# Cross attention over 1500 keys: the values' quarter loads by an order of lanes on fifteen DMA engines, the residual's load and the result's store in slots of their own

## The chip, the cores and the metric

One core of one Trainium2 chip runs the whole program. The metric is the device time of one execution in microseconds (us); lower is better. Engines are named as the profile names them: PE (TensorE's matmuls), PEld (its weight loads), DVE (VectorE), ACT (ScalarE), POOL (GpSimd) and SP (SyncE, which issues every DMA here; SPq are its rows). The core has 16 DMA engines.

## The reference

32 samples (batches b), 56 queries and 1500 keys each, hidden size 512, 32 heads of 16. Keys and values are the same tensor `ctx`.

```python
x = (hidden - mean) * rsqrt(var + 1e-5) * gamma + beta        # layer norm over 512
Q = split_heads(x @ Wq.T); K = V = split_heads(ctx)
scores = einsum('bhsd,bhtd->bhst', Q, K) * HEAD_DIM ** -0.5
probs = softmax(where(mask, scores, -inf))                    # mask (32, 1500)
attn = einsum('bhst,bhtd->bhsd', probs, V)
out = hidden + merge_heads(attn) @ Wout.T
```

## The kernel before

**Tiles.** The 1500 keys of a batch are CHUNKS = 3 chunks of 500, and a chunk is CHUNK = 4 quarters of LANES = 125 keys, one key to a partition ("lane"). A batch has thus SLOTS = 12 slots, slot k being quarter k % 4 of chunk k // 4. The host hands the keys over transposed (`kt`) and the mask in two layouts; the values are read from `ctx` as it is: lane m of quarter k of a chunk is key 4m + k, a row of 512 floats (2048 bytes).

**The work of a slot on PE** (lines 718 to 737): four bf16 score tiles that run ahead for the next batches' maxima (`score_tile`, line 268), four matmuls that put in minus the maximum (`begin_scores`, line 301), the slot's scores in fp32 (`score_blocks`, line 309), and the product of the slot before with the values (`times_values`, line 325). DVE adds the mask to each ahead tile and takes its maximum (line 347), ACT makes the exponentials (lines 391 and 393), POOL copies a chunk's values from `v_stage` into the spread layout `v` (`spread_values`, line 435, once for four slots). Every second batch PE projects the output of a pair of batches in four parts (`project_out`, line 284), and DVE adds the residual `x_res` and leaves the sum in `result` (`add_residual`, line 364). The places are fixed in OUT_AT = [(2, 9), (3, 3), (3, 9), (4, 3)]: batches after the pair's first, and the slot.

**The work is unrolled.** The program is straight code: 40,736 matmuls with as many weight loads. There is no loop on an engine.

**SP's order** (lines 512 to 530). Before each slot SP waits until the values' product of the slot before is done (`pv_done`), then issues one quarter of the keys for two batches ahead (`load_k`, line 222: 128 partitions of 2000 bytes), one quarter of the values for the next chunk (`load_v`, line 233: 125 partitions of 2048 bytes), in slots 1, 4 and 7 a chunk of the mask (`load_mask`, line 237: 112 partitions of 1000 bytes), and in slot 4 of every even batch the result's store (`store_result`, line 247) and the residual's load (`load_residual`, line 243), both 112 rows of 2048 bytes. `v_stage` has two stages; all four quarters of a stage add 16 each to `v_landed`, for which POOL waits at line 431.

```python
if k == CHUNK and b % 2 == 0 and b > 0:
    if b > 2:
        store_result(sp, b // 2 - 2)
    load_residual(sp, b // 2 - 1)
```

Of the kernel before, what the change touches and what calls it, by code (L numbers as in the profile page):

```python
# [11 lines left out]
BATCH, QUERIES, HIDDEN = 32, 56, 512  # L12
# [6 lines left out]
BLOCKS, TILES_R, ROW = 4, 4, 32  # L19
# [2 lines left out]
BANK_Q = BLOCKS * PAIR_Q  # L22
CHUNKS, CHUNK, LANES = 3, 4, 125
SLOTS = CHUNKS * CHUNK
KEYS = CHUNK * LANES
MAX_TILES = CHUNKS * PAIRS
AHEAD = 8
# [3 lines left out]
STAGES = 2  # L31
# [42 lines left out]
def slot_units(b, k):  # L74

    tiles = slot_tiles(b, k)
    return tiles[0:3] + slot_rows(b, k) + tiles[3:4] + slot_others(b, k)
# [3 lines left out]
RING = FIRST_TILES + [("rows", 0)]  # L81
RING += [unit for b in range(BATCH) for k in range(SLOTS) for unit in slot_units(b, k)]
LAST_OUTS = [("out", d, part) for d in range(BATCH // 2 - 2, BATCH // 2) for part in range(OUT_PARTS)]
# [5 lines left out]
def build(nc, x, kt, ctx, mask_lanes, mask_rows, wq_t, wout_t, gamma, beta, out):  # L89
    with ExitStack() as stack:  # L90
        def sb(name, shape, dt=F32):
            return stack.enter_context(nc.sbuf_tensor(name, shape, dt))

        def sem(name):
            return stack.enter_context(nc.semaphore(name))
# [4 lines left out]
        v_stage = sb("v_stage", [128, STAGES, CHUNK, HIDDEN])  # L100
# [5 lines left out]
        woutT = sb("woutT", [128, BLOCKS, HIDDEN])  # L106
        mask_bias = sb("mask_bias", [128, BATCH * SLOTS])
        mask_tile = sb("mask_tile", [128, 2, CONTEXT], BF16)
        masked = sb("masked", [128, len(RING_BANKS), KEYS], BF16)
        tile_max = sb("tile_max", [128, CHUNKS, PAIRS])  # L110
# [22 lines left out]
        ln_weights = sb("ln_weights", [128, 2, BLOCKS])  # L133
        lanes_u8 = sb("lanes_u8", [128, BATCH * SLOTS], U8)
        rows_u8 = sb("rows_u8", [BATCH, CONTEXT], U8)
# [6 lines left out]
        def x_tile(t):  # L142
            if t < 14:
# [3 lines left out]
              for i in range(2)]  # L147
        wqT = v_scratch[:, 2 * BLOCKS * BANK_Q:2 * BLOCKS * BANK_Q + BLOCKS * HIDDEN].rearrange("p (c n) -> p c n",
                                                                                              c=BLOCKS)
# [23 lines left out]
        v_landed = [sem(f"v_landed{i}") for i in range(STAGES)]  # L173
# [27 lines left out]
        def wait_over(eng, semaphore, count):  # L201
            if count > 0:
                eng.wait_ge(semaphore, count)
# [4 lines left out]
        def wait_taken(eng, unit):  # L208
            eng.wait_ge(ring_taken, RING_AT[unit] + 1)
# [11 lines left out]
        def load_k(sp, b, c, g):  # L221
            sp.dma_start(kT[:, b % 2, c, g].rearrange("p k m -> p (k m)"), kt[b, c, :, KEYS * g:KEYS * (g + 1)]
                         ).then_inc(k_landed[b % 2][c], 16)
# [3 lines left out]

        def load_v(sp, b, c, k):
            n = CHUNKS * b + c
            src = ctx[b, KEYS * c:KEYS * (c + 1), :].rearrange("(m k) n -> m k n", k=CHUNK)  # L230
            if k == 0:
                wait_over(sp, v_ready, n - STAGES + 1)
            sp.dma_start(v_stage[0:LANES, n % STAGES, k], src[:, k]).then_inc(v_landed[n % STAGES], 16)

        def load_mask(sp, b, c):
            keys = slice(KEYS * c, KEYS * (c + 1))
            sp.dma_start(mask_tile[0:PAIR_Q, b % 2, keys], mask_add[b:b + 1, keys].broadcast_to([PAIR_Q, KEYS])
                         ).then_inc(mask_tile_landed[b % 2], 16)
# [6 lines left out]
        def store_result(sp, d):  # L245
            wait_taken(sp, ("out", d, OUT_PARTS - 1))
            sp.dma_start(out_rows[d], result[0:PAIR_Q, :]).then_inc(result_stored, 16)
# [8 lines left out]
        def score_tile(pe, unit):  # L256
# [5 lines left out]
            if t % PAIRS == 0:  # L262
# [4 lines left out]
            keys = keys.rearrange("p (n h) -> p n h", h=2)[:, :, 1]  # L267
            nc.tensor.matmul(bank[0:PAIR_Q, 0:KEYS], qdb[rows, b % 2, g, :], keys,  # L268
                             start=True, stop=True).then_inc(ring_filled, 1)
# [19 lines left out]
        def begin_scores(pe, b, k):  # L289
# [3 lines left out]
            if k == 0:  # L293
                pe.wait_ge(rows_spread, b + 1)
                pe.wait_ge(qd_ready, b + 1)
            n = SLOTS * b + k
            wait_over(pe, exped_held, n)
# [7 lines left out]
        def score_blocks(pe, b, k, blocks):  # L305
            for g in blocks:
                for r in range(TILES_R):
                    rows = slice(ROW * r, ROW * (r + 1))
                    mm = nc.tensor.matmul(ps[0:LANES, score_bank(SLOTS * b + k, r), PAIR_Q * g:PAIR_Q * (g + 1)],  # L309
                                          kT[rows, b % 2, k // CHUNK, g, k % CHUNK, :], qd[rows, b % 2, g, :],  # L310
# [4 lines left out]
        def times_values(pe, b, k):  # L315
            c = k // CHUNK
            if k % CHUNK == 0:
                pe.wait_ge(v_ready, CHUNKS * b + c + 1)
            pe.wait_ge(exped, SLOTS * b + k + 1)
            if k == 0:  # L320
# [107 lines left out]
        def spread_values(pool, b, c):  # L428

            n = CHUNKS * b + c  # L430
            pool.wait_ge(v_landed[n % STAGES], 16 * CHUNK * (n // STAGES + 1))
            wait_over(pool, pv_done, CHUNK * (n - CHUNKS + 1))
            halves = v[0:LANES, c].rearrange("p k i (h d) -> p (k i) h d", d=HEAD_DIM)[:, :, 0:3:2, :]
            staged = v_stage[0:LANES, n % STAGES].rearrange("p k (i h d) -> p (k i) h d", h=2, d=HEAD_DIM)
            nc.gpsimd.tensor_copy(halves, staged).then_inc(v_ready, 1)  # L435
# [33 lines left out]
        @block.sync  # L469
        def _(sp):  # L470
            def load_x(u):
                for t in range(UNIT_AT[u], UNIT_AT[u] + UNIT_TILES[u]):
                    sp.dma_start(x_tile(t), x_rows[t]).then_inc(x_landed[u], 16)

            load_x(0)
            for n, weight in enumerate((gamma, beta)):
                sp.dma_start(ln_weights[:, n, :], weight.rearrange("(c p) -> p c", p=128),
                             allow_slow_non_contiguous=True).then_inc(ln_landed, 16)
            sp.dma_start(wqT, wq_t.rearrange("(c p) n -> p c n", p=128)).then_inc(wq_landed, 16)
            sp.dma_start(rows_u8[:, :], mask_rows).then_inc(mask_landed, 16)  # L480
            sp.dma_start(lanes_u8[0:LANES, :], mask_lanes).then_inc(mask_landed, 16)
            load_x(1)
            for g in range(BLOCKS):
                load_k(sp, 0, 0, g)
            for u in range(2, UNITS):
                load_x(u)
            for g in range(BLOCKS):
                load_k(sp, 0, 1, g)
            for g in range(BLOCKS):
                load_k(sp, 0, 2, g)  # L490
            sp.wait_ge(mask_added, 1)
            sp.dma_start(mask_add, rows_add[:, :]).then_inc(mask_stored, 16)
            for g in range(BLOCKS):
                load_k(sp, 1, 0, g)
            sp.wait_ge(mask_stored, 16)
            for c in range(CHUNKS):
                load_mask(sp, 0, c)
            for c in range(CHUNKS):
                load_mask(sp, 1, c)
            for k in range(CHUNK):  # L500
                load_v(sp, 0, 0, k)
            sp.dma_start(woutT[:, :, :], wout_t.rearrange("(c p) n -> p c n", p=128)).then_inc(wout_landed, 16)
            for g in range(BLOCKS):
                load_k(sp, 1, 1, g)
            for g in range(BLOCKS):
                load_k(sp, 1, 2, g)
            sp.wait_ge(filled, FILLS)
            for k in range(CHUNK):
                load_v(sp, 0, 1, k)
            for k in range(CHUNK):  # L510
                load_v(sp, 0, 2, k)
            for b in range(BATCH):
                for k in range(SLOTS):
                    step = k % CHUNK
                    wait_over(sp, pv_done, SLOTS * b + k)
                    if (b, k) >= (0, CHUNK):
                        of, c = (b + 2, k // CHUNK - 1) if k >= CHUNK else (b + 1, CHUNKS - 1)
                        if of < BATCH:
                            load_k(sp, of, c, step)
                        of, c = (b + 1, k // CHUNK - 1) if k >= CHUNK else (b, CHUNKS - 1)  # L520
                        if of < BATCH:
                            load_v(sp, of, c, step)
                    if k in (1, 4, 7) and b + 2 < BATCH:
                        if k == 1:
                            wait_taken(sp, ("tile", b, MAX_TILES - 1))
                        load_mask(sp, b + 2, k // 3)
                    if k == CHUNK and b % 2 == 0 and b > 0:
                        if b > 2:
                            store_result(sp, b // 2 - 2)
                        load_residual(sp, b // 2 - 1)  # L530
            store_result(sp, BATCH // 2 - 2)
            load_residual(sp, BATCH // 2 - 1)
            store_result(sp, BATCH // 2 - 1)
            sp.wait_ge(result_stored, 16 * (BATCH // 2))
# [249 lines left out]
```

## Time and profile before

| | us |
|---|---|
| median of 3 runs | 1495.26 (1488.03 to 1503.92) |
| profiled execution | 1497.4 |
| its span, first to last instruction | 1495.6 |
| granted TensorE clock over the span | 0.963 |
| PE busy / PEld / DVE | 1352.0 / 1037.6 / 1088.4 |
| ACT / POOL | 769.7 / 388.8 |

The span is 1.8 us shorter than the execution's own time. Busy times are sums over the span; the clock is a share of 2.4 GHz, and it is granted at one of two levels, 2.4 or 1.2 GHz. An idle time is put down to what ended it; "issue" is an idle time for which the profile shows nothing that was waited for.

### The profile page before, as it was taken

How to read it: one execution, taken by the hardware profiler on the slowest of the kernel's cores; microseconds unless marked ns; L12 is line 12 of the kernel's file. 1: busy time of each engine (PE TensorE's matmuls, PEld its weight loads, DVE VectorE, ACT ScalarE, POOL GpSimd, SP SyncE). 2: the span in 40 equal slices, each digit the busy share in tenths (PEclk: the TensorE clock that was granted, in tenths of full speed). 3: DMA queues.
4: the chain of work that ended last, by engine and by line, in shares of the span. 5: the costliest groups of instructions: out<-in, count | busy, mean ns of one | idle time of the engine just before them, and what ended most of it. 6: DMA issues, size and time to landing. Idle time of an engine off the chain costs nothing.

```text
span 1495.6 us, 88664 instructions
## 1 busy us (share of the span) xinstructions
PE 1352.0 (90%) x40736; PEld 1037.6 (69%) x40736; DVE 1088.4 (73%) x3452; ACT 769.7 (51%) x847; POOL 388.8 (26%) x371
## 2 busy tenths in 40 slices
PE   6999989999999989999999989989998998889986
PEld 4347777777667777777777767767776777677775
DVE  6657778788777777877777877878786777777640
ACT  2126555555555555555455555555554554555463
POOL 1011323332322233322222332322223222223221
PEclk8999999999999999999999999999999999999899
DMA  8314555555545544555555554555555444454430
GB/s 271 99 38 150 163 160 160 161 159 159 166 152 162 166 156 154 161 163 158 156 158 173 162 161 150 167 153 161 170 166 153 145 151 158 147 170 145 131 98 21
DMA packets 126358, 226.37 MB, mean 151 GB/s; under 512 B 11619, under 2 KB 71555, under 8 KB 125987
## 3 DMA queue, kind: packets, MB, share of 16 engines
q1 hardware_dynamic: 125986, 220.71, 47.7%
q8 instruction: 320, 5.24, 1.5%
q14 instruction: 52, 0.42, 0.1%
HBM read 216.90 MB, written 3.77 MB: 148 GB/s over the span
## 4 chain that ended last, share of the span: by engine, by line
PE 66%; DVE 26%; issue 6%; ACT 2%; DMA 0%; POOL 0%; SPq 0%; POOLq 0%; DVEq 0%; ACTq 0%
DVE masked L347 22%; PE ps L325 22%; PE ps L268 21%; PE ps L309 12%; PE ps L284 5%; PE ps L707 4%; PE ps L301 2%; DVE den_inv L383 2%; ACT probs L391 1%; PE ps L275 1%; DVE tile_max L347 1%; DMA v<-in_wq_t 0%; DVE probs L612 0%; PE ps L698 0%; DVE den L376 0%
## 5 line engine op out<-in xcount | busy, mean ns | idle before, releaser
L347 DVE CUSTOM_DVE_ANT_0 masked<-ps,mask_tile 112x500 bf16<-112x500 f32 x1536 | 974.1, 674 | 327.4 <-PE ps L268 315.1
L391 ACT ACTIVATE probs<-ps,mask_bias 125x1344 f32<-125x1344 f32 x384 | 530.6, 1382 | 629.6 <-PE ps L309 629.6
L268 PE MATMUL ps<-kT,qdb 32*112 32x500 bf16 x1536 | 496.6, 423 | 45.5 <-DVE tile_max L347 35.8
L309 PE MATMUL ps<-qd,kT 32*125 32x112 f32 x12288 | 478.7, 277 | 13.6 <-issue 13.4
L309 PEld LDWEIGHTS ps<-qd,kT 32*125 32x125 f32 x12288 | 475.1, 190 | 21.7 <-issue 18.0
L325 PE MATMUL ps<-probs,v 125*32 125x56 f32 x24576 | 410.4, 218 | 38.0 <-issue 36.1
L325 PEld LDWEIGHTS ps<-probs,v 125*32 125x32 f32 x24576 | 343.7, 113 | 132.7 <-issue 125.5
L268 PEld LDWEIGHTS ps<-kT,qdb 32*112 32x112 bf16 x1536 | 156.3, 125 | 208.2 <-DVE tile_max L347 158.9
L393 ACT ACTIVATE probs<-ps,mask_bias 125x448 f32<-125x448 f32 x384 | 240.7, 627 | 0.0
L435 POOL COPY v<-v_stage 125x2048 f32<-125x2048 f32 x96 | 181.7, 1892 | 201.1 <-DMA v_stage<-in_ctx 201.1
L301 PE MATMUL ps<-max_rows,ones_row 4*125 4x448 bf16 x1536 | 213.7, 391 | 7.9 <-ACT probs L391 5.5
L424 POOL TENSOR_TENSOR max_rows<-rows,own_block 128x448 bf16<-128x448 f32 x32 | 29.9, 934 | 613.3 <-DVE rows L370 613.3
L347 DVE DVE_READ_ACCUMULATOR2_ANT tile_max<- 112x1 f32 x1536 | 127.9, 83 | 0.0
L464 POOL TENSOR_TENSOR attnT<-heads,den_inv 128x224 f32<-128x224 f32 x32 | 21.1, 658 | 248.3 <-DVE den_inv L383 248.3
L284 PE MATMUL ps<-woutT,attnT 128*112 128x128 f32 x512 | 74.2, 291 | 7.5 <-POOL attnT L464 4.8
L284 PEld LDWEIGHTS ps<-woutT,attnT 128*112 128x112 f32 x512 | 61.7, 183 | 22.3 <-DVE tile_max L347 11.6
L301 PEld LDWEIGHTS ps<-max_rows,ones_row 4*125 4x125 bf16 x1536 | 64.5, 132 | 15.3 <-ACT probs L391 6.7
L707 PE MATMUL ps<-v 128*128 128x448 f32 (+2 forms) x160 | 66.1, 534 | 2.5 <-DMA v<-in_wq_t 1.5
L383 DVE RECIPROCAL den_inv<-den 128x56 f32<-128x56 f32 x128 | 63.1, 496 | 0.2
L364 DVE TENSOR_TENSOR result<-ps,x_res 112x128 f32<-112x128 f32 x64 | 18.6, 291 | 40.0 <-PE ps L284 36.6
L672 ACT COPY qT<-ps 128x448 f32<-128x448 f32 (+2 forms) x20 | 9.1, 457 | 64.6 <-PE ps L707 64.5
L707 PEld LDWEIGHTS ps<-v 128*128 128x128 f32 x160 | 27.5, 216 | 18.2 <-issue 12.5
(48 smaller groups left out, 295.6 us busy)
## 6 DMA issues: line engine op xcount, KB each, us to landing
kT<-in_kt SPq DMA_DIRECT2D x384, 250.0 KB, 3.1
v_stage<-in_ctx SPq DMA_DIRECT2D x384, 250.0 KB
mask_tile<-mask_add SPq DMA_DIRECT2D x96, 109.4 KB, 4.5
x_res<-in_x SPq DMA_DIRECT2D x16, 224.0 KB, 5.6
out<-result SPq DMA_DIRECT2D x16, 224.0 KB, 5.4
probs<-in_x SPq DMA_DIRECT2D x14, 224.0 KB, 8.4
v<-in_wq_t SPq DMA_DIRECT2D x1, 1024.0 KB, 6.0
woutT<-in_wout_t SPq DMA_DIRECT2D x1, 1024.0 KB, 16.9
```

Source lines behind the costliest of these rows:

```text
L268: nc.tensor.matmul(bank[0:PAIR_Q, 0:KEYS], qdb[rows, b % 2, g, :], keys, start=True, stop=True).then_inc(ring_filled, 1)
L284: mm = nc.tensor.matmul(bank[0:PAIR_Q, 0:OUT_COLS], attnT[:, d % 2, g, :], woutT[:, g, OUT_COLS * part:OUT_COLS * (part + 1)], start=(g == ...
L301: nc.tensor.matmul(ps[0:LANES, score_bank(n, r), 0:BANK_Q], ones_row[rows, :], max_rows[rows, b % 2].rearrange("p g n -> p (g n)"), start= ...
L309: mm = nc.tensor.matmul(ps[0:LANES, score_bank(SLOTS * b + k, r), PAIR_Q * g:PAIR_Q * (g + 1)], kT[rows, b % 2, k // CHUNK, g, k % CHUNK, ...
L325: mm = nc.tensor.matmul(acc[ROW * r:ROW * (r + 1), i, :], v[0:LANES, c, k % CHUNK, TILES_R * g + r, HEAD_DIM * e:HEAD_DIM * e + ROW], prob ...
L347: nc.vector.tensor_tensor_reduce(out=sums, in0=bank[0:PAIR_Q, 0:KEYS], in1=mask_tile[0:PAIR_Q, b % 2, KEYS * c:KEYS * (c + 1)], scale=1.0, ...
L383: nc.vector.reciprocal(den_inv[:, g], den[:, g]).then_inc(den_inverted, 1)
L391: nc.scalar.activation(probs[0:LANES, k % PROBS, 0:HELD_ROWS], ps[0:LANES, 0:HELD_ROWS, 0:BANK_Q], ACT.Exp, bias=bias, scale=SCALE).then_i ...
L393: nc.scalar.activation(probs[0:LANES, k % PROBS, HELD_ROWS], ps[0:LANES, score_bank(n, HELD_ROWS), 0:BANK_Q], ACT.Exp, bias=bias, scale=SC ...
L424: nc.gpsimd.tensor_tensor(max_rows[:, b % 2], rows[:].unsqueeze(1).broadcast_to([128, BLOCKS, PAIR_Q]), own_block[:].unsqueeze(2).broadcas ...
L435: nc.gpsimd.tensor_copy(halves, staged).then_inc(v_ready, 1)
L707: mm = nc.tensor.matmul(bank, wqT[:, h, 128 * c:128 * (c + 1)], xT[u % 2][:, h, 0:w], start=(h == 0), stop=(h == BLOCKS - 1))
```

## The change

The 125 lanes of a quarter are put in another order. The first 120 are read as 8 rows of 15: lane a*8 + j holds the key row that was lane 15j + a; the last five stay. So a quarter's load becomes two DMAs: one with a source of 15 x 8 rows for lanes 0 to 119, and one for lanes 120 to 124. The host puts the transposed keys and both layouts of the mask in the same order. `v_landed` now gets 32 per quarter. SP issues the store in slot 5 and the residual's load in slot 6, in place of both in slot 4.

```diff
+VALUE_RINGS = 15
+EVEN_LANES = LANES // VALUE_RINGS * VALUE_RINGS
+LANE_OF = [m for a in range(VALUE_RINGS) for m in range(a, EVEN_LANES, VALUE_RINGS)] + list(range(EVEN_LANES, LANES))
...
         def load_v(sp, b, c, k):
             n = CHUNKS * b + c
-            src = ctx[b, KEYS * c:KEYS * (c + 1), :].rearrange("(m k) n -> m k n", k=CHUNK)
+            src = ctx[b, KEYS * c:KEYS * (c + 1), :].rearrange("(m k) n -> m k n", k=CHUNK)[:, k]
+            even = src[0:EVEN_LANES].rearrange("(j a) n -> a j n", a=VALUE_RINGS)
             if k == 0:
                 wait_over(sp, v_ready, n - STAGES + 1)
-            sp.dma_start(v_stage[0:LANES, n % STAGES, k], src[:, k]).then_inc(v_landed[n % STAGES], 16)
+            sp.dma_start(v_stage[0:EVEN_LANES, n % STAGES, k], even).then_inc(v_landed[n % STAGES], 16)
+            sp.dma_start(v_stage[EVEN_LANES:LANES, n % STAGES, k], src[EVEN_LANES:LANES]
+                         ).then_inc(v_landed[n % STAGES], 16)
...
-            pool.wait_ge(v_landed[n % STAGES], 16 * CHUNK * (n // STAGES + 1))
+            pool.wait_ge(v_landed[n % STAGES], 2 * 16 * CHUNK * (n // STAGES + 1))
...
-                    if k == CHUNK and b % 2 == 0 and b > 0:
-                        if b > 2:
-                            store_result(sp, b // 2 - 2)
+                    if k == CHUNK + 1 and b % 2 == 0 and b > 2:
+                        store_result(sp, b // 2 - 2)
+                    if k == CHUNK + 2 and b % 2 == 0 and b > 0:
                         load_residual(sp, b // 2 - 1)
...
-    keys = ctx.reshape(BATCH, CHUNKS, LANES, CHUNK, BLOCKS, 128)
-    lanes = mask.reshape(BATCH, CHUNKS, LANES, CHUNK)
+    keys = ctx.reshape(BATCH, CHUNKS, LANES, CHUNK, BLOCKS, 128)[:, :, LANE_OF]
+    lanes = mask.reshape(BATCH, CHUNKS, LANES, CHUNK)[:, :, LANE_OF]
```

## Rows read from the trace of the kernel before

**Rows 1.** The page: busy times, and the chain that ended last by engine.

```profile
PE 1352.0 (90%) x40736; PEld 1037.6 (69%) x40736; DVE 1088.4 (73%) x3452; ACT 769.7 (51%) x847; POOL 388.8 (26%) x371
...
PE 66%; DVE 26%; issue 6%; ACT 2%; DMA 0%; POOL 0%; SPq 0%; POOLq 0%; DVEq 0%; ACTq 0%
```

**Rows 2.** Waits: engine line <- releaser, us in total, times, longest us.

```profile
POOL v L435 <- DMA v_stage<-in_ctx: 201.1, 36, 30.0
PEld ps L325 <- issue: 125.5, 388, 2.8
PE ps L325 <- issue: 36.1, 44, 2.7
PE ps L309 <- issue: 13.4, 24, 2.3
PE ps L301 <- issue: 2.1, 3, 1.1
```

**Rows 3.** Engines by stretch: the whole loop, then four single batches.

```profile
core 0: us, PE busy (x) PEld busy (x) DVE busy (x) ACT busy (x) POOL busy (x), PEclk, DMA share, GB/s
161.40:1415.40 1254.00, 1147.83 (x36586) 901.76 (x36585) 957.78 (x3059) 673.43 (x723) 346.32 (x318) 0.97 0.52 158
...
933.90:974.30 40.40, 37.95 (x1267) 29.80 (x1267) 32.93 (x107) 23.34 (x26) 11.97 (x11) 1.00 0.53 165
974.30:1019.90 45.60, 40.83 (x1267) 31.81 (x1266) 33.24 (x107) 23.41 (x26) 11.97 (x11) 0.93 0.52 156
1019.90:1061.40 41.50, 39.02 (x1267) 30.41 (x1266) 33.31 (x107) 23.25 (x26) 11.97 (x11) 1.00 0.51 161
1326.40:1371.90 45.50, 40.17 (x1267) 31.84 (x1266) 33.39 (x107) 23.27 (x26) 12.01 (x11) 0.96 0.49 156
```

**Rows 4.** Timeline of PE: first, one middle and last of eleven stalls.

```profile
208.89 1.53 PE L325 MATMUL ps<-probs,v 125*32 125x56 f32 x55 [2.66 <-issue]
...
725.98 0.62 PE L325 MATMUL ps<-probs,v 125*32 125x56 f32 x19 [1.42 <-issue]
...
1156.96 1.41 PE L309 MATMUL ps<-qd,kT 32*125 32x112 f32 x21 [2.33 <-issue]
```

**Rows 5.** The page: DMA queues, packets, MB, share of 16 engines.

```profile
q1 hardware_dynamic: 125986, 220.71, 47.7%
q8 instruction: 320, 5.24, 1.5%
```

**Rows 6.** Timeline of SP around the stall at 724.56 us.

```profile
718.08 0.35 SPq L222 DMA_DIRECT2D kT<-in_kt  x1
718.47 0.33 SPq L233 DMA_DIRECT2D v_stage<-in_ctx  x1
718.84 0.32 SPq L237 DMA_DIRECT2D mask_tile<-mask_add  x1
719.20 0.43 SPq L247 DMA_DIRECT2D out<-result  x1
719.97 0.33 SPq L243 DMA_DIRECT2D x_res<-in_x  x1
721.75 0.35 SPq L222 DMA_DIRECT2D kT<-in_kt  x1
722.15 0.33 SPq L233 DMA_DIRECT2D v_stage<-in_ctx  x1
```

**Rows 7.** Engines by short stretch: values alone; burst's middle; burst's end; after the stall.

```profile
715.90:716.90 1.00, 1.00 (x35) 0.89 (x31) 0.97 (x3) 0.00 (x0) 0.00 (x0) 1.00 0.32 123
...
720.40:721.90 1.50, 1.50 (x71) 1.15 (x75) 1.09 (x4) 1.50 (x2) 1.50 (x2) 1.00 0.46 147
722.20:723.20 1.00, 1.00 (x37) 0.75 (x29) 1.00 (x3) 0.00 (x0) 0.12 (x1) 1.00 0.86 243
...
725.90:733.00 7.10, 7.02 (x157) 6.21 (x159) 3.86 (x12) 1.91 (x2) 0.00 (x0) 0.52 0.44 128
```

**Rows 8.** DMA issues: KB each, median us from issue to landing.

```profile
kT<-in_kt SPq DMA_DIRECT2D x384, 250.0 KB, 3.1
v_stage<-in_ctx SPq DMA_DIRECT2D x384, 250.0 KB
mask_tile<-mask_add SPq DMA_DIRECT2D x96, 109.4 KB, 4.5
x_res<-in_x SPq DMA_DIRECT2D x16, 224.0 KB, 5.6
out<-result SPq DMA_DIRECT2D x16, 224.0 KB, 5.4
```

**Rows 9.** Timeline of SP in a stretch with no stall.

```profile
961.19 0.35 SPq L222 DMA_DIRECT2D kT<-in_kt  x1
961.58 0.33 SPq L233 DMA_DIRECT2D v_stage<-in_ctx  x1
964.26 0.35 SPq L222 DMA_DIRECT2D kT<-in_kt  x1
964.65 0.33 SPq L233 DMA_DIRECT2D v_stage<-in_ctx  x1
```

## The prediction

> **What bounds the kernel now.** I read the page first. PE is busy 90% of the span, DVE 73%, and the chain that ended last is 66% PE, 26% DVE, 6% "issue" and 0% DMA [rows 1]. By that view a change to loads is worth nothing: no engine on the chain waits for a transfer, and POOL, which does wait 201.1 us for the values, is busy 26% and copies four slots ahead of need [rows 1, 2]. So the question became what the 6% of issue is, some 90 us in which PE waited for nothing that the profile shows.
>
> The second view was the loop by batches. The issue of the keys' load in slot 4 marks each batch; from 161.4 to 1415.4 us there are 29 of them. One (933.9 to 974.3) took 40.40 us at a full clock; the next 45.60 us at a clock of 0.93, with the same instructions and the same busy time on DVE, ACT and POOL [rows 3]. So 40.4 us is what the code needs by its own waits, and 29 x 40.4 = 1171.6 us against 1254.0 leaves 82.4 us of disturbance in the loop. That is what a change to DMAs can reach.
>
> The third view was PE's timeline in the bad batches. Eleven times PE stops for 1.24 to 2.66 us, mostly in the middle of a run of matmuls of one line, where there is no semaphore to wait for [rows 4]. Then the granted clock is at its lower level for a stretch: 725.9 to 733.0 us shows 0.52 [rows 7], 1.2 GHz for nearly all of it. All idle time of PE before a matmul that is put down to issue sums to 36.1 + 13.4 + 2.1 = 51.6 us [rows 2]. The loop's clock of 0.97 [rows 3] is (1 - 0.97) x 1254 = 38 us of work done late. 52 + 38 = 90 us, the size of the 82 found by batches.
>
> **What PE waits for there.** The program is straight code, and the page has a queue of kind instruction: 320 packets, 5.24 MB, thus 16.4 KB each [rows 5]. PE and PEld have 81,472 instructions [rows 1], 255 to a packet. PE's code thus comes by DMA, a block every 4 us or so, and a stop within a run of one line is a block that is late. The trace names no engine for it, so this is an inference.
>
> The Trainium skill ("Runtime: NRT & Kernel Launch", Instruction fetch mechanics) says the same of the size, 16 KiB blocks of 256 instructions, and that crossing one is mostly hidden. By that rule the stops are something else and the time would stay where it is; the rows with stops of up to 2.66 us inside a run speak against "hidden" in this program, so I give it a small chance below.
>
> Why late? Ten of the eleven stops come in the slot after the one in which SP issues keys, values, mask, result and residual in a row (the first without a result yet), the eleventh one slot later; one such burst stands at 718.08 to 719.97 us, and its stop from 724.56 to 725.98 [rows 4, 6]. The DMA share tells more. While only a quarter of values moves, the engines' mean share is 0.32 at 123 GB/s: five of sixteen [rows 7]. 250 KB at 123 GB/s is 2.1 us on those five. In the burst's middle (720.4 to 721.9) the share is still only 0.46, though mask, result and residual have been issued and go over all engines; only when the values are through does it rise to 0.86 [rows 7]. So what stands behind the values in SP's queue is let out at the pace of the five engines while others idle, and SP itself is held: the residual is issued 0.77 us after the result where neighbours are 0.37 apart [rows 6]. The code block, I think, is held up in the same jam. The mask's 109 KB take 4.5 us to land against 3.1 for the keys' 250 KB [rows 8]: the same jam, small, in three slots of each batch.
>
> **The change part by part.**
>
> *Values on fifteen engines.* The Trainium skill ("DMA: Bandwidth & Descriptors", Why a DMA increments its semaphore by 16 and not by 1) has the engine count as the largest divisor up to 16 of both sides' slowest dimension: 5 for 125, 15 for 15 x 8 rows into 120 partitions. The trace agrees on the 5.
> If the split works, a quarter has 8 rows to an engine in place of 25, and 2.1 x 8/25 = 0.7 us in place of 2.1. The last five lanes add one row on each of some engines, under 0.1 us. The jam behind the values goes, in every slot.
>
> *One more issue per slot on SP.* 384 more issues at 0.33 us plus the gap, about 0.37 us each. A slot's issues become 0.4 + 0.4 + 0.4 + 0.4 (mask) = 1.6 us within a slot of 3.08 us in which nothing disturbs (keys at 961.19 and at 964.26) [rows 9]. SP waits for the rest anyway. On the path: 0. If SP were to fall behind, values land four slots before their use and keys a batch before; the cover is over 10 us. Bounds: 0 to 2 us. The larger count at line 431 costs nothing.
>
> *Order of lanes.* Host work, and the same rows in SBUF; softmax sums over lanes in another order. PE, DVE, ACT and POOL issue what they did. 0.
>
> *Store in slot 5, residual in slot 6.* Neither slot has a mask. The residual is used in slot 9, three slots or 9 us later, and takes 5.6 us [rows 8]; the result's store takes 5.4 us and `result` is written again in slot 9. Both hold. The moved pair no longer stands with the mask behind one set of values: 2.1 us on five engines plus three transfers become, per slot, keys and values and one transfer of at most 224 KB over 16 engines. Nothing new is waited for; 0 on SP.
>
> *Sum.* The eleven long stops are 21.6 us (2.66 + 1.72 + 1.75 + 1.24 + 2.59 + 1.56 + 1.42 + 1.25 + 2.57 + 2.50 + 2.33; first and last in [rows 4]). The lower clock, 38 us, follows them; the batch from 1019.9 to 1061.4 us, with short stops alone, has 1.00 [rows 3]. I take all of the stops and 32 of the 38, since a few lower stretches may stay: 54 us. The short stops are 51.6 - 21.6 = 30 us, of which some 6 lie in head and tail; late batches such as 1326.4 to 1371.9 (45.50 us) are full of them [rows 3]. Those behind a mask or a tail of values should go; those behind the keys' load, which takes all 16 engines as before, stay. I take a third off, 8 us. 1497.4 - 54 - 8 = 1435.4; for the second issue and new meetings I add 3 and say 1438 us. The profiled run is 2.1 us above the median of three, within their spread of 16 us, so nothing is taken off for that. Both ends: all 82 us gone and some more in head and tail gives 1412; nothing gained gives 1497.
>
> **The rivals.**
>
> 1. *Only the long stops' worst part goes.* If the code block is delayed by any busy engines, and the jam is only part of it, keys and values together still hold it. Then stops shrink from 2 to 1 us and half of the clock comes back: 1497 - 11 - 19 = 1467 us. For it: short stops occur in batches without store or residual [rows 3]. Against: the batch at 933.9 has five-engine values throughout and no loss.
>
> 2. *No effect.* Either the load stays on five engines, or the stops belong to the fetch itself, whatever else moves. 1490 to 1500 us. For it: 0% of the chain is DMA [rows 1], and one long stop, at 208.89 us, has no store before it. Against: the stops' place, one slot after the burst.
>
> 3. *Slower.* The code block comes over engines that values do not touch today; from the change on they carry 0.7 us of values behind 0.7 to 1 us of keys in each slot. If a block waits for both, every one is up to 0.7 us later. Where the slack is gone (PE stopped before a matmul 44 + 24 + 3 = 71 times [rows 2] for 320 blocks), that is some 80 x 0.5 us = 40 us more, partly met by what the moved store and residual give (20 us): 1517 us. It decides if the block's engine serves SP's packets first; for it speaks that the values' own stretch shows no sign of sharing, 0.32 at 123 GB/s; against it, that DMA share is 0.53 on the mean and a block moves 16 KB in about 1.1 us (1.5% x 16 x 1495.6 / 320) [rows 5].
>
> **How the numbers follow.** The forecast with 1412 to 1455 us gets 0.60, rival 1 0.19, rival 2 0.13, rival 3 0.08. The range of 8 in 10 is 1410 to 1482. About 1% is what a measurement of this kernel can tell from no change; faster by more takes the forecast and nearly all of rival 1: 0.79; within 1% 0.14; slower 0.07.
>
> **What would show it.** Right: while only values move, a DMA share near 0.9 for 0.7 us in place of 0.32 for 2.1; two issues of `v_stage` to a slot; the mask landing in about 3 us in place of 4.5; PE's idle time from issue before a matmul from 51.6 to under 25 us; the loop's clock at 0.99 or more; batches of 40.4 to 42 us, even and odd alike; DVE, ACT and POOL busy as before. Wrong: stops of over 1.2 us that stay in the slots after 4, 5 or 6 of even batches (rival 1 or 2), or more short stops in every batch and a block's packet time well over 1.1 us (rival 3).

## The result: slower by 1.9%, and the profile after

The changed kernel takes 1524.76 us (median of 4 runs, 1517.77 to 1532.55) against 1497.78 for the one before in the same comparison: ratio 1.0188, 95% interval 1.0107 to 1.0268. The forecast was 1438 with a range of 1410 to 1482; the result lies outside it, on the other side of no change. The profiled execution took 1528.94 us, its span 1526.7. Ratios here and below leave out executions over 1.5% above the fastest one of the same kernel (none of these four, five of the ten of padded below), medians do not.

From the page of the changed kernel: busy times, queues, the chain by engine, DMA issues with the median us to landing.

```profile
PE 1360.0 (89%) x40736; PEld 1040.7 (68%) x40736; DVE 1087.7 (71%) x3452; ACT 770.0 (50%) x847; POOL 388.5 (25%) x371
...
q1 hardware_dynamic: 131746, 220.73, 52.0%
q8 instruction: 320, 5.24, 1.4%
...
PE 66%; DVE 24%; issue 7%; ACT 1%; DMA 0%; POOL 0%; SPq 0%; POOLq 0%; DVEq 0%; ACTq 0%
...
kT<-in_kt SPq DMA_DIRECT2D x384, 250.0 KB, 3.3
v_stage<-in_ctx SPq DMA_DIRECT2D x384, 240.0 KB
mask_tile<-mask_add SPq DMA_DIRECT2D x96, 109.4 KB, 3.5
v_stage<-in_ctx SPq DMA_DIRECT2D x384, 10.0 KB
x_res<-in_x SPq DMA_DIRECT2D x16, 224.0 KB, 4.0
out<-result SPq DMA_DIRECT2D x16, 224.0 KB, 3.4
```

The engines do the same work [rows 1]. Mask, residual and result land 1.0, 1.6 and 2.0 us sooner than before [rows 8], as forecast. The packets grew by 5760 = 384 x 15 [rows 5], and the trace has them as packets of 4 bytes, 11,493 before and 17,253 now. That fits one such packet from each engine that takes part in a DMA: a quarter now ends on 15 + 5 in place of 5 engines, and the spread does what it says. But the same 220.7 MB keep the sixteen engines busy for 52.0% of a longer span in place of 47.7%.

The waits of PE and SP (engine line <- releaser, us in total, times, longest us); L331 and L315 are the values' product and the scores, [rows 2] of before.

```profile
POOL v L441 <- DMA v_stage<-in_ctx: 181.3, 37, 23.7
PEld ps L331 <- issue: 149.9, 426, 2.6
PE ps L331 <- issue: 53.9, 75, 2.4
PE ps L315 <- issue: 14.7, 30, 1.0
PE ps L307 <- issue: 2.1, 4, 1.1
```

PE's idle time before a matmul for which the profile shows nothing was 51.6 us in 71 stops; it is 53.9 + 14.7 + 2.1 = 70.7 us in 109. They are a little shorter (0.65 us on the mean against 0.73) and far more. They make up 19.1 of the 31.1 us by which the span grew; PE's busy time, 1360.0 against 1352.0, makes up 8.0. Three batches of after and the whole loop by stretch show the same, as [rows 3] did.

```profile
core 0: us, PE busy (x) PEld busy (x) DVE busy (x) ACT busy (x) POOL busy (x), PEclk, DMA share, GB/s
164.40:1400.40 1236.00, 1115.29 (x35436) 872.98 (x35440) 928.02 (x2966) 652.66 (x700) 335.00 (x308) 0.98 0.57 156
204.50:251.90 47.40, 41.86 (x1267) 32.89 (x1266) 33.29 (x107) 23.16 (x26) 12.01 (x11) 0.93 0.54 146
1008.00:1049.30 41.30, 38.58 (x1267) 29.84 (x1266) 33.09 (x107) 23.44 (x26) 11.96 (x11) 1.00 0.61 173
1354.20:1400.40 46.20, 39.57 (x1270) 30.86 (x1273) 33.79 (x109) 23.81 (x27) 11.99 (x11) 1.00 0.57 154
```

The last of these batches runs at a full clock and still takes 46.20 us: PE's idle time put down to issue is 4.6 us in it and 0.3 us in the one at 1008.0. The best one takes 41.30, the best before 40.40. The loop's clock is 0.98 against 0.97, so the clock is not what made the kernel slower; nor did it come back to 0.99, where I had counted on 32 of its 38 us.

What became of a quarter of values is read from 702.4 to 704.2 us of after, in two parts and whole, with SP's issues around it, and from a later quarter with no mask behind it (709.9 to 711.4 us).

```profile
702.40:703.10 0.70, 0.68 (x26) 0.45 (x30) 0.70 (x3) 0.70 (x1) 0.70 (x2) 1.00 0.72 50
703.10:704.20 1.10, 1.10 (x68) 1.02 (x59) 0.51 (x3) 0.94 (x2) 1.10 (x1) 1.00 0.71 253
702.40:704.20 1.80, 1.78 (x77) 1.47 (x80) 1.21 (x5) 1.64 (x2) 1.80 (x2) 1.00 0.71 174
709.90:711.40 1.50, 1.50 (x79) 1.39 (x82) 0.91 (x5) 1.34 (x2) 0.00 (x0) 1.00 0.48 150
```

```profile
700.16 0.36 SPq L225 DMA_DIRECT2D kT<-in_kt  x1
700.57 1.23 SPq L237 DMA_DIRECT2D v_stage<-in_ctx  x1
701.83 0.47 SPq L238 DMA_DIRECT2D v_stage<-in_ctx  x1
702.36 0.32 SPq L243 DMA_DIRECT2D mask_tile<-mask_add  x1
703.83 0.35 SPq L225 DMA_DIRECT2D kT<-in_kt  x1
704.23 0.87 SPq L237 DMA_DIRECT2D v_stage<-in_ctx  x1
705.14 0.46 SPq L238 DMA_DIRECT2D v_stage<-in_ctx  x1
```

For 0.7 us 72% of the engines are busy and move 50 GB/s: many have begun a row and few bytes arrive. The quarter takes some 1.8 us, not 0.7. Its second part is not the values' alone: the mask issued at 702.36 starts to move at 703.6 us, and without a mask the share is 0.48. The cost in engine time is better read from the trace's packets over the whole loop (165 to 1400 us). A packet of 2048 bytes, nearly always a row of values, takes 116.5 ns on the mean against 89.5 before; the median is 84 in both, so it is a tail of slow ones. A quarter's 125 rows thus hold 14.6 us of engine time in place of 11.2. The queue's shares agree: 0.520 x 16 x 1526.7 us is 1288 us more than 0.477 x 16 x 1495.6, 3.4 us for each of the 384 quarters. I had counted 0.7 us on fifteen engines, no more engine time than before. The issue itself went from 0.33 us to 0.87 + 0.47, which the experiments had to clear or convict.

### The profile page after: what moved, and what is told of

Read it like the earlier page. It is cut to its first block, busy times and chain, and to the rows that moved or that the text cites. A ratio compares the mean times of both kernels' runs of the same rounds, so it can differ in the third digit from the quotient of the medians.

```text
span 1526.7 us, 89048 instructions
## 1 busy us (share of the span) xinstructions
PE 1360.0 (89%) x40736; PEld 1040.7 (68%) x40736; DVE 1087.7 (71%) x3452; ACT 770.0 (50%) x847; POOL 388.5 (25%) x371
## 2 busy tenths in 40 slices
DMA packets 132120, 226.41 MB, mean 148 GB/s; under 512 B 17378, under 2 KB 77314, under 8 KB 131746
## 3 DMA queue, kind: packets, MB, share of 16 engines
q1 hardware_dynamic: 131746, 220.73, 52.0%
## 4 chain that ended last, share of the span: by engine, by line
PE 66%; DVE 24%; issue 7%; ACT 1%; DMA 0%; POOL 0%; SPq 0%; POOLq 0%; DVEq 0%; ACTq 0%
PE ps L331 22%; DVE masked L353 22%; PE ps L274 20%; PE ps L315 12%; PE ps L290 5%; PE ps L713 4%; PE ps L307 2%; DVE den_inv L389 1%; PE ps L281 1%; ACT probs L397 1%; DVE tile_max L353 1%; DMA v<-in_wq_t 0%; PE ps L704 0%; DVE probs L618 0%; DVE den L382 0%
## 5 line engine op out<-in xcount | busy, mean ns | idle before, releaser
L274 PE MATMUL ps<-kT,qdb 32*112 32x500 bf16 x1536 | 492.9, 421 | 47.7 <-DVE tile_max L353 39.8
L315 PE MATMUL ps<-qd,kT 32*125 32x112 f32 x12288 | 480.6, 276 | 14.8 <-issue 14.7
L315 PEld LDWEIGHTS ps<-qd,kT 32*125 32x125 f32 x12288 | 475.8, 189 | 24.1 <-issue 20.5
L331 PE MATMUL ps<-probs,v 125*32 125x56 f32 x24576 | 419.6, 218 | 56.1 <-issue 53.9
L331 PEld LDWEIGHTS ps<-probs,v 125*32 125x32 f32 x24576 | 347.2, 112 | 157.6 <-issue 149.9
```

What stands on the lines that cost most here:

```text
L331: mm = nc.tensor.matmul(acc[ROW * r:ROW * (r + 1), i, :], v[0:LANES, c, k % CHUNK, TILES_R * g + r, HEAD_DIM * e:HEAD_DIM * e + ROW], prob ...
```

## The experiments

Ratios are against the kernel before, timed on the same chip in the same comparison. "Idle" is PE's idle time before matmuls put down to issue, the values', the scores' and the maximum's lines summed from each profile as above.

| kernel | engines for the values' bulk, rows' order, DMAs per quarter | ratio (95% interval) | median us | idle us |
|---|---|---|---|---|
| before | 5, old, 1; slot 4 | 1 | | 51.6 |
| after | 15, changed, 2 | 1.0188 (1.0107 to 1.0268) | 1524.76 | 70.7 |
| slots | 5, old, 1 | 0.9852 (0.9799 to 0.9905) | 1480.99 | 38.7 |
| rings | 15, changed, 2; slot 4 | 1.0280 (1.0214 to 1.0346) | 1543.12 | 82.2 |
| natural | 15, old, 2 | 1.0079 (1.0030 to 1.0129) | 1512.90 | 53.9 |
| five_two | 5, changed, 2 | 1.0188 (1.0131 to 1.0245) | 1529.43 | 69.5 |
| one_plain | 15, old, 1 | 1.0079 (1.0044 to 1.0114) | 1510.72 | 54.2 |
| one_3d | 15, changed, 1 | 1.0196 (1.0123 to 1.0269) | 1533.57 | 71.8 |
| narrow | 15, changed, 2, 1/8 of the bytes | 0.9694 (0.9650 to 0.9739) | 1456.67 | 32.6 |
| five_plain | 5, old, 2 | 0.9861 (0.9810 to 0.9911) | 1481.54 | 36.2 |
| ten | 10, old, 2 | 0.9824 (0.9770 to 0.9879) | 1471.00 | 34.7 |
| eleven | 11, old, 2 | 0.9915 (0.9878 to 0.9952) | 1492.18 | 42.6 |
| thirteen | 13, old, 2 | 0.9996 (0.9964 to 1.0028) | 1502.14 | 50.0 |
| split15 | 15, old, 2 | 1.0041 (0.9998 to 1.0085) | 1503.29 | 57.0 |
| split5 | 15 (meant: 5), old, 2 | 0.9998 (0.9954 to 1.0042) | 1501.82 | 55.8 |
| padded | 15, near old, 2, form kept | 1.0022 (0.9978 to 1.0066) | 1511.91 | 55.0 |
| keys_eleven | 10, old, 2; keys on 11 | 0.9931 (0.9886 to 0.9976) | 1492.72 | 42.4 |
| whole_keys | 5, old, 1; keys once a chunk | 1.0381 (1.0307 to 1.0456) | 1554.83 | 74.9 |
| apart15 | 15, old, 2; half a slot later | 1.0132 (1.0092 to 1.0173) | 1526.86 | 63.1 |
| apart10 | 10, old, 2; half a slot later | 1.0020 (0.9978 to 1.0063) | 1507.71 | 55.4 |

All but "before" and the "slot 4" row have the store and the residual in slots 5 and 6. In five_plain the last ten lanes are a DMA of their own, on ten engines by the count of packets. The idle column goes with the ratio nearly all the way: a kernel whose loads cost more has more stops of PE that the profile cannot put down to a semaphore. They are not the whole difference. PE's busy time moves too, from 1329.5 us in narrow to 1378.2 in rings, while the granted clock of the span goes from 0.988 to 0.950. natural, split15 and split5 came out as the same loads (below) and gave 1.0079, 1.0041 and 0.9998 in two comparisons, so steps of less than about 0.008 between kernels of different comparisons say little.

**Half and half.** The change has two parts; each was run alone.

slots:

```diff
-                    if k == CHUNK and b % 2 == 0 and b > 0:
-                        if b > 2:
-                            store_result(sp, b // 2 - 2)
+                    if k == CHUNK + 1 and b % 2 == 0 and b > 2:
+                        store_result(sp, b // 2 - 2)
+                    if k == CHUNK + 2 and b % 2 == 0 and b > 0:
                         load_residual(sp, b // 2 - 1)
```

> The kernel before with only the store moved to slot 5 and the residual's load to slot 6. Jam theory (transfers behind the five-engine values hold the code block): the stops after even batches' slot 4 shrink, 1465 to 1480 us, ratio 0.98 to 0.99. Rival (the move itself is harmful or idle): ratio 1.00 or above.

rings is the changed kernel with these lines as they were.

> The changed kernel with store and residual back in slot 4: fifteen engines alone. If the fifteen engines carry the whole loss and the slots gain: above the changed kernel, 1535 to 1550 us. If the slots carry the loss: 1500 us or below.

The slots gain 1.5%, some 22 us, and the values' load loses it and more, with or without them: 1.0280 against 1, 1.0188 against 0.9852. The two parts add within their intervals. In the trace of slots the longest stop before a values' matmul is 1.6 us against 2.7 before.

```profile
PE ps L325 <- issue: 22.6, 46, 1.6
PE ps L309 <- issue: 13.0, 23, 1.1
PE ps L301 <- issue: 3.1, 5, 1.1
```

```profile
mask_tile<-mask_add SPq DMA_DIRECT2D x96, 109.4 KB, 4.6
x_res<-in_x SPq DMA_DIRECT2D x16, 224.0 KB, 5.9
out<-result SPq DMA_DIRECT2D x16, 224.0 KB, 4.9
```

Mask and residual land no sooner in slots than before (4.5 and 5.6 us there; the result took 5.4), and it gains all the same; the changed kernel lands all three sooner and loses. The time to landing is no measure of what the code meets on the engines.

**What in the values' load?** Three things had changed at once: engines, order of rows with a dearer issue, and a second DMA.

natural (changed kernel, two lines):

```diff
-LANE_OF = [m for a in range(VALUE_RINGS) for m in range(a, EVEN_LANES, VALUE_RINGS)] + list(range(EVEN_LANES, LANES))
+LANE_OF = list(range(LANES))
...
-            even = src[0:EVEN_LANES].rearrange("(j a) n -> a j n", a=VALUE_RINGS)
+            even = src[0:EVEN_LANES]
```

> The changed kernel with the lanes in their old order: lanes 0 to 119 as a plain block of 120 rows, and lanes 120 to 124. If 120 rows also go over fifteen engines with an issue of 0.33 us in place of 0.87, issue theory (the code block waits while SP's issues are made into descriptors): 1495 to 1510 us. Engine theory (values on the block's own engine hold it): 1520 to 1530 us like the changed kernel.

five_two (changed kernel with 5 for VALUE_RINGS and 120 for EVEN_LANES):

> The changed kernel with 5 in place of 15 (24 rows to an engine, the last five lanes in a second DMA as there): the dear form and the second issue stay, the spread goes. Issue theory: 1515 to 1530 us like the changed kernel. Engine theory: the ratio of the kernel with moved slots alone, 0.98 to 1.00.

Changed order, dear form and second DMA on five engines cost as much as the whole load on fifteen, 1.0188, and natural, with its cheaper issues, lies between. That read as a win for the issue theory, by which the code waits while SP makes its issues. The issues' own durations (min/median/max ns): natural, then five_two.

```profile
L237 SPq DMA_DIRECT2D v_stage<-in_ctx x384: 324/440/1887, 31.8 to 1473.0; - x192
L238 SPq DMA_DIRECT2D v_stage<-in_ctx x384: 289/299/690, 32.3 to 1473.3; - x192
```

```profile
L237 SPq DMA_DIRECT2D v_stage<-in_ctx x384: 753/759/896, 35.7 to 1487.5; - x192
L238 SPq DMA_DIRECT2D v_stage<-in_ctx x384: 477/487/772, 36.6 to 1488.3; - x192
```

**The issue theory tested.** one_plain and one_3d drop the second DMA from natural and from the changed kernel:

```diff
-            sp.dma_start(v_stage[EVEN_LANES:LANES, n % STAGES, k], src[EVEN_LANES:LANES]
-                         ).then_inc(v_landed[n % STAGES], 16)
+            if n < STAGES:
+                sp.dma_start(v_stage[EVEN_LANES:LANES, n % STAGES, k], src[EVEN_LANES:LANES]
+                             ).then_inc(v_landed[n % STAGES], 16)
```

The count that POOL waits for follows. Both kernels leave out the last five lanes of every quarter after the first two chunks, 4% of the values' bytes.

> Natural order, fifteen engines, one DMA per quarter: lanes 120 to 124 are loaded for the first two chunks alone and keep their old values later (4% of the values' bytes left out). Issue theory (SP 0.35 + 0.44 us a slot): 1481 to 1492 us, like the kernel with moved slots alone. Engine theory: 1505 to 1515 us, like the natural order with both DMAs.

> The changed kernel's order of lanes, one DMA per quarter, lanes 120 to 124 left out after the first two chunks. If SP's time per issue decides (0.35 + 0.87 = 1.22 us a slot): 1500 to 1512 us. If the number of issues decides: 1481 to 1492 us. If the spread over engines decides: 1520 us.

five_plain is natural with EVEN_LANES = 115:

> Moved slots, natural order, each quarter as lanes 0 to 114 and lanes 115 to 124: the bulk stays on five engines, one plain issue of some 0.3 us is added. Issue theory: 1500 to 1515 us, as the natural order on fifteen engines. If the second issue costs nothing by itself: 1475 to 1485 us.

narrow is the changed kernel with

```diff
+            cols = slice(0, HIDDEN if n < STAGES else HIDDEN // 8)
-            sp.dma_start(v_stage[0:EVEN_LANES, n % STAGES, k], even).then_inc(v_landed[n % STAGES], 16)
+            sp.dma_start(v_stage[0:EVEN_LANES, n % STAGES, k, cols], even[:, :, cols]).then_inc(v_landed[n % STAGES], 16)
```

and the same columns in the second DMA. It leaves out 7/8 of the values' bytes after the first two chunks.

> The changed kernel with the same DMAs and rows, but after the first two chunks only the first 64 of 512 columns of each value row are loaded (256 bytes in place of 2048; the other columns keep old values). Issue theory: 1515 to 1530 us, unchanged. Traffic theory (the bytes on the engines hold the code block): below 1495 us.

Here the issue theory fell. A second issue is free: one_plain equals natural (1.0079 both), one_3d equals the changed kernel, five_plain equals slots. narrow keeps every issue at its full price and is the fastest kernel of the study, with the loop's clock at 1.00. The rows that decide: narrow's issues, its queue and its loop.

```profile
L238 SPq DMA_DIRECT2D v_stage<-in_ctx x384: 872/882/1892, 33.0 to 1417.6; - x192
L239 SPq DMA_DIRECT2D v_stage<-in_ctx x384: 457/468/614, 34.1 to 1418.5; - x192
```

```profile
q1 hardware_dynamic: 131746, 136.50, 34.8%
```

```profile
161.40:1400.00 1238.60, 1147.56 (x37327) 895.48 (x37327) 976.33 (x3125) 686.73 (x737) 348.17 (x320) 1.00 0.37 99
```

So it is what the values' bytes do on the engines. One_plain and five_plain have the same plain form and differ in the spread of the bulk: 15 engines cost 0.022 more than 5.

**How many engines?** ten, eleven and thirteen are natural with EVEN_LANES at 100, 121 and 117.

> Moved slots, natural order, plain form, each quarter as lanes 0 to 99 on ten engines (10 rows each) and 100 to 124 on five. Engine theory with the code block on one of the upper five that the values reach at fifteen (10 to 14): ratio 0.985 as on five engines. With the block on one of 5 to 9: 1.008 as on fifteen. With the block's engine changing from block to block: about 0.997.

> Moved slots, natural order, lanes 0 to 120 on eleven engines (11 rows each), 121 to 124 on four. One-engine theory: 0.982 as on ten, unless the code's engine is the eleventh, then 1.005. Slope theory (each further engine costs a little): about 0.987.

> Lanes 0 to 116 on thirteen engines (9 rows each), 117 to 124 on eight. One-engine theory: 0.982 if the code's engine is the 14th or 15th, 1.005 if it is the 11th to 13th. Slope theory: about 0.996.

Ten engines cost nothing (0.9824, within the interval of five). Then it climbs: 0.9915 and 0.9996, in one comparison and with intervals that do not meet, and 1.0049 as the mean of natural, one_plain, split15 and split5, the old order on fifteen. The last step, from thirteen to fifteen, is within what such kernels differ by. Eleven lies between the 0.987 of the slope theory and the 1.005 of a single engine that is the eleventh; thirteen, which is above eleven, speaks for the slope. The number of rows to an engine and the second DMA's engines change along with the count, so the slope is one of all three. keys_eleven asks the same from the other side, taking the keys off the upper engines too:

```diff
-            sp.dma_start(kT[:, b % 2, c, g].rearrange("p k m -> p (k m)"), kt[b, c, :, KEYS * g:KEYS * (g + 1)]
-                         ).then_inc(k_landed[b % 2][c], 16)
+            for lo, hi in ((0, 110), (110, 128)):
+                sp.dma_start(kT[lo:hi, b % 2, c, g].rearrange("p k m -> p (k m)"), kt[b, c, lo:hi, KEYS * g:KEYS * (g + 1)]
+                             ).then_inc(k_landed[b % 2][c], 16)
```

> Values on ten engines as in the run of that name, and the keys' quarter in two DMAs, partitions 0 to 109 on eleven engines (10 rows each), 110 to 127 on nine. If the code's engine is the 12th to 15th it now carries mask, result and residual alone: most stops go, clock 0.99, 1420 to 1445 us. If it is the 11th, or if any engine's traffic holds the code: 1465 to 1480 us.

The count that PE waits for follows. 1492.72 us is 0.011 above ten and above both of the ranges given: taking the keys off the upper engines gained nothing. It also adds an issue to each slot and puts more on the engines that are left, so it tells only that no upper engine is worth keeping free of keys; with the slope it is against a single one.

**The order of rows.** split15 and split5 read `"(a j) n -> a j n"` in place of `"(j a) n -> a j n"`; padded does so with one row of padding after every eight in the source, so that the form stays.

> The changed kernel, its three-dimensional form of source kept (15 x 8 rows), but each engine reads eight neighbouring rows, so the lanes stay in their old order. If the form costs (SP 0.87 us an issue): 1.019 as the changed kernel. If the order of addresses costs: 1.008 as the plain form on fifteen. Should SP's issue come back to 0.44 us the form has been folded and only the latter can be seen.

> The same on five engines (5 x 24 neighbouring rows and five lanes). Form theory: 1.019 as with the changed order on five engines. Address theory: 0.985 as the plain form on five.

> The changed kernel's two DMAs on fifteen engines with its 15 x 8 form kept by one row of padding after every eight in the values' source; each engine reads neighbouring rows. Form theory: 1.019 as the changed kernel. Address theory: 1.005 as the natural order on fifteen.

Both splits were folded back into the plain form: their issues take 435 and 436 ns like natural's, and both count 131746 packets, the number of fifteen engines, split5 too. So neither tells form from addresses, and split5 is a third run of natural's loads, which is why it stands at 15 in the table. padded tells it: its issue takes 883 ns, as the changed kernel's, and its ratio is 1.0022.

```profile
L237 SPq DMA_DIRECT2D v_stage<-in_ctx x384: 872/883/1867, 31.5 to 1464.7; - x192
```

On fifteen engines the form is free, and the changed order of addresses costs: 1.0188 and 1.0196 against 0.9998 to 1.0079. (The padding moves the rows' addresses too; which property of them counts is not shown.) On five engines the order with its form costs 0.033 (five_two against five_plain); there the form was not tried apart. And with the changed order fifteen engines are no dearer than five, 1.0188 both. So spread and order do not add: the order with its form, alone on five engines, brings the whole loss of 0.033, and the spread alone 0.020 of it.

**Is it the length of a burst?** whole_keys loads a chunk's keys at once, in rows of 8000 bytes (K_STEP is 2; the count that PE waits for follows):

```diff
-            sp.dma_start(kT[:, b % 2, c, g].rearrange("p k m -> p (k m)"), kt[b, c, :, KEYS * g:KEYS * (g + 1)]
+            if g != K_STEP:
+                return
+            sp.dma_start(kT[:, b % 2, c].rearrange("p g k m -> p (g k m)"), kt[b, c]
                          ).then_inc(k_landed[b % 2][c], 16)
```

> Moved slots, values as before on five engines; the keys of a chunk come in one DMA of 1 MB (8000 bytes a partition) in place of four, issued at the third of its four slots. If the keys' 16-engine bursts of 1.1 us in every slot are what is left of the stops: fewer stops but longer ones, 1450 to 1480 us. If a long burst holds a block for all of its 3 us: 1490 to 1520 us.

1554.83 us, the slowest of all and above its rival's range of 1490 to 1520: one burst of 1 MB in four slots, with a quarter of the issues, is worse than four of 250 KB. apart15 and apart10 go the other way and part keys and values:

```diff
                         if of < BATCH:
+                            sp.wait_ge(scored, SLOTS * b + k + 2)
                             load_v(sp, of, c, step)
```

> Natural order on fifteen engines, but SP waits for the next slot's scores between the keys' and the values' issue, some 1.4 us. If the joined stretch of keys and values holds the code: ratio down from 1.005 to 0.985 or below. If the amount of traffic decides: 1.00 to 1.008, unchanged.

> The same on ten engines. Joined stretch: from 0.982 down to 0.965 to 0.975. Amount: 0.98 to 0.985. Should the wait make values late, POOL's wait for them would pass 250 us and PE would wait for the spread values.

Both lost, 0.008 and 0.020 against their parents (1.0049 and 0.9824), and both lie above everything expected of them; the first difference is at the edge of what comparisons differ by. Two separate bursts per slot are worse than one joined, though the wait also holds back mask, result and residual. So the joined stretch is not what costs; a longer burst (whole_keys) and more bursts (apart) both do, fewer bytes help (narrow).

**What the stops wait for.** The kept traces hold the packets of the queue "instruction" with their times, 320 of 16 KB [rows 5], and these settle it for the long stops. In the loop of the kernel before (165 to 1400 us) PE stops, with neither a matmul nor a weight load, for more than 1.2 us eleven times. Each of these stops ends 1.2 to 1.6 us after such a packet has ended, and the next packet starts 1.1 to 1.8 us after the stop. Over the 20 kernels there are 146 such stops, and each ends 1.2 to 1.8 us behind a packet's end, where a packet starts only every 4.2 us at the median. So a long stop is PE waiting for its code, and it ends when a block has come. There are 11 before, 9 in after, 13 in rings, 11 in five_two, 21 in whole_keys, and one each in slots, ten and narrow. (The many shorter stops are not sorted out as cleanly.)

The delay lies ahead of the packet and not in it. The eleven late packets take 1.04 us on the mean, those of the whole loop 1.12, but they start 5.9 to 7.1 us after the one before them, against the median of 4.2. In the 1.5 us before they start, the loads' packets keep the engines 87% busy, against 50% before an average code packet (77% against 54% in after). Over all 20 kernels it is 76% against 52%. The reading that fits all of this, though no run isolates it, is that a code packet has to wait for quiet engines, and each arrangement of the loads leaves more or less of them. What it waits for there, a descriptor, an engine's turn or memory, and over which engines it comes, no run here tells.

## Why the prediction was wrong

**What bounds the kernel: right.** The disturbance was in PE's unexplained stops, and they moved the time in both directions, from 0.9694 to 1.0381, with DMA at 0 or 1% of the chain throughout. That they are waits for code was an inference from the size and number of the packets; for the long ones the packets' times show it. The Trainium skill ("Runtime: NRT & Kernel Launch", Instruction fetch mechanics) calls this cost mostly hidden; by these rows it is not in this program, where 220 MB of loads run beside straight code.

**Slots 5 and 6: right.** They gain 1.5% alone, within the 0.98 to 0.99 expected of them, and leave one stop of over 1.2 us of eleven. The burst of five transfers in one slot was the trouble, as the prediction has it.

**The jam: right as a fact, wrong as the cause.** Mask, residual and result do land sooner. But in the spread kernels no time followed from it. The step that failed is "The code block, I think, is held up in the same jam": that the five engines' stretch of values holds the code, so that ending it early gives back 54 + 8 us. The runs show the reverse: with the old order, fifteen engines cost 30 us over five, and with the changed order nothing was gained by them. Under it lies a second failed step, "if the split works, a quarter has 8 rows to an engine in place of 25, and 2.1 x 8/25 = 0.7 us". The quarter read above took some 1.8 us, and a quarter holds 14.6 us of engine time in place of 11.2, as a row takes 116.5 ns in place of 89.5; I had kept the engine time as a constant. What I had read as waste, eleven idle engines for 2 us of each slot, was probably of use: the runs with ten to fifteen engines say so, though none shows which engine brings the code.

**The terms.** Spread to fifteen: +2.0% or 30 us (1.0049 against 0.985 for five), forecast as part of a gain of 62. Order of rows: +1.4% or 21 us (1.0188 against 1.0049), forecast 0: the prediction calls it "Host work" and leaves out that the engines read other addresses. Slots: -22 us. The sum, +29 us, meets the measured 1524.76 - 1497.78 = 27. It does so by the path taken: with the order changed first, on five engines, order and form cost 49 us (1.0188 against 0.9861) and the spread then 0. Only their sum, some 50 us, is firm. The second issue, for which I had set 0 to 2 us, is free, as costed. That last point is worth its place: SP's 1.7 us per slot looked like a culprit and was none.

**The rivals.** Rival 3 came nearest, at a chance of 0.08: more stops, each short, 1517 us; there were 38 more stops and 1524.76 us. That the number is so near is partly luck: it had +40 for the spread and nothing for the order. Its argument, that values would reach engines that the code had to itself, fits the runs from ten to fifteen engines in the old order. It does not explain five_two, which loses the same on five engines, and one of its signs did not come: a code packet takes 1.08 us on the mean and not well over 1.1 (1.12 before). The code comes late and not slowly. I ranked the rival low because the batch at 933.9 us ran well with the spread as it was, which spoke for the five engines and not for fifteen. Of my signs for a right forecast the mask's landing came near (3.5 us for about 3); the DMA share near 0.9 for 0.7 us, the loop's clock of 0.99 and the idle time (under 25 us forecast, 70.7 found) did not come. The idle time tells the two apart at one look.

## What to carry to other kernels

A transfer that nobody waits for can still set the time through the engines it keeps busy: before spreading a load, ask who else uses the engines that it does not touch, the program's own code included, and read the idle time that the profile puts down to issue. Spread only as far as it helps: here ten engines with plain rows and the slots moved is the best that was built, 1471.00 us (0.9824), 3.6% under the changed kernel by their ratios, though its interval meets those of five engines. Where one edit bundles a count, an order and a form, try each by itself; here the part that looked dear (SP's issues) was free, and one that looked free (the order of rows) cost 21 us on fifteen engines. Where a stop of PE has no releaser, lay its end beside the packets of the instruction queue.

## What was not expected of the hardware

- PE stops while a block of its own code is late: each stop of over 1.2 us ends 1.2 to 1.8 us after a 16 KB packet of the instruction queue has ended, 146 of 146 in 20 kernels, and those packets start late (5.7 us after the one before at the median, against 4.2 for all) but are hardly longer (1.14 us on the mean against 1.12).
- The order in which rows are dealt to engines costs time with the same bytes, engines and row length: 1.0188 against 1.0022 on fifteen engines with equal issue times of some 0.88 us.
- An issue with a three-dimensional source of 15 x 8 rows takes 0.87 to 0.88 us against 0.44 for 120 plain rows and 0.33 for 125; the five rows' issue takes 0.47 beside the former and 0.30 beside the latter. Nor is it the form's alone: in apart15, where 120 plain rows are not issued right behind the keys, they take 0.33.
- One DMA of 1 MB in place of four of 250 KB made the kernel 5.4% slower than slots (1.0381 against 0.9852) with 288 fewer issues, its rows 8000 bytes in place of 2000: fewer issues are no gain in themselves.
- The number of packets tells the number of engines of a DMA. The counts fit one packet of 4 bytes for every engine of each: 384 loads on fifteen and five engines in place of five add 384 x 15 = 5760.
